# Dealing the steps of an expert lookup over the units of a decoder block's last part

## The reference

```python
q = jnp.einsum('bnd,de->bne', x, w_q)
mean = jnp.mean(q, axis=(0, 1)); var = jnp.var(q, axis=(0, 1))
q = (q - mean) * jax.lax.rsqrt(var + BN_EPS) * bn_gamma + bn_beta
q = q.reshape(b, n, 2, H, KD).transpose(2, 0, 1, 3, 4)
sim = jnp.einsum('pbnhd,hkpd->pbnhk', q, keys)
sx, ix = jax.lax.top_k(sim[0], TOPK)
sy, iy = jax.lax.top_k(sim[1], TOPK)
all_scores = (sx[..., :, None] + sy[..., None, :]).reshape(b, n, H, TOPK * TOPK)
all_indices = (ix[..., :, None] * NUM_KEYS + iy[..., None, :]).reshape(b, n, H, TOPK * TOPK)
scores, pk = jax.lax.top_k(all_scores, TOPK)
indices = jnp.take_along_axis(all_indices, pk, axis=-1)
wd = down_embed[indices]
wu = up_embed[indices]
h = gelu_new(jnp.einsum('bnd,bnhkd->bnhk', x, wd))
h = jax.nn.softmax(scores, axis=-1) * h
out = jnp.einsum('bnhk,bnhkd->bnd', h, wu)
```

## Time and profile before

| | us |
|---|---|
| median of 3 runs | 2746.43 (2737.4 to 2747.01) |
| profiled execution | 2732.75, span 2730.9 |
| first gather issued | 1358.2 |
| gathers of head 7 begin | 2555.1 |
| last gather issued | 2714.4 |
| TensorE busy | 2356.3 (86%) |
| VectorE busy | 1869.2 (68%) |
| ScalarE busy | 1176.5 (43%) |
| GpSimd busy | 1144.1 (42%) |

### The profile page before, as it was taken

How to read it: one execution, slowest core, us unless ns; L and a number is a source line. 1 busy time by engine, 2 the same in 40 slices (tenths; PEclk the granted TensorE clock), 3 DMA queues, 4 the chain that set the end, 5 groups by cost and what they waited for, 6 DMA issues and landing times.

```text
span 2730.9 us, 37792 instructions
## 1 busy us (share of the span) xinstructions
PE 2356.3 (86%) x12444; PEld 1259.1 (46%) x12444; DVE 1869.2 (68%) x5474; ACT 1176.5 (43%) x3224; POOL 1144.1 (42%) x1082
## 2 busy tenths in 40 slices
PE   8999999999999999998868888778878788876767
PEld 4565555656555565655534433333333343332323
DVE  4676777777687777768467767677775766766554
ACT  3365574736557473657223423323333332332222
POOL 3111212111121211120166576676667666577665
PEclk9999999999999999999989999989899998898889
DMA  4001001010100101011189899999999999899998
GB/s 175 30 1 37 8 8 37 1 44 1 41 4 10 36 1 43 1 60 58 58 320 364 299 369 357 349 354 345 358 352 363 351 362 358 309 359 356 355 375 330
DMA packets 161954, 521.78 MB, mean 191 GB/s; under 512 B 17248, under 2 KB 27488, under 8 KB 161760
## 3 DMA queue, kind: packets, MB, share of 16 engines
q0 software_dynamic: 129024, 469.82, 45.8%
q1 hardware_dynamic: 31152, 48.03, 5.3%
q10 hardware_dynamic: 1584, 1.52, 0.2%
HBM read 508.30 MB, written 11.01 MB: 190 GB/s over the span
## 4 chain that ended last, share of the span: by engine, by line
PE 20%; issue 10%; DVE 10%; another core or an unknown queue 3%; POOL 3%; DMA 3%; ACT 1%; DVEq 1%; POOLq 0%; ACTq 0%
PE ps_y L1819 7%; PE ps_o L1819 7%; DVE e_rows L1965 5%; PE ps_s L1789 3%; POOL e_rows L1769 3%; DMA e_rows<-in_experts,e_idx 3%; PE ps_t L1802 1%; ACT e_diag L2047 1%; DVE acc L1955 1%; DVE e_at L1899 1%; DVE e_best_at L1879 1%; DVEq L1903 0%; DVE q_stats L1847 0%; ACT e_q_t L2022 0%
## 5 line engine op out<-in xcount | busy, mean ns | idle before, releaser
L1769 POOL DMA_INDIRECT e_rows<-in_experts,e_idx x896 | 908.6, 1014 | 473.0 <-issue 284.6
L1965 DVE CUSTOM_DVE_ANT_0 e_rows<-e_rows,xn_all 128x512 f32<-128x512 f32 x896 | 568.6, 688 | 148.4 <-DMA e_rows<-in_experts,e_idx 112.5
L1819 PE MATMUL ps_o<-e_rows,e_diag 128*128 128x512 f32 x896 | 443.1, 642 | 149.2 <-issue 131.3
L1819 PE MATMUL ps_y<-e_rows,e_diag 128*128 128x512 f32 x896 | 434.5, 632 | 121.6 <-ACT e_diag L2047 60.4
L2047 ACT ACTIVATE e_diag<-ident_f,e_weight 128x128 f32<-128x128 f32 x896 | 286.3, 390 | 560.5 <-DVE e_weight L1976 197.1
L1819 PEld LDWEIGHTS ps_o<-e_rows,e_diag 128*128 128x128 f32 x896 | 179.8, 206 | 384.7 <-issue 362.5
L1819 PEld LDWEIGHTS ps_y<-e_rows,e_diag 128*128 128x128 f32 x896 | 178.1, 203 | 355.1 <-issue 316.1
L1133 DVE SCALAR_TENSOR_TENSOR ring<-ps_s,mask 112x750 f32<-112x750 f32 x248 | 225.0, 936 | 129.2 <-PE ps_s L624 110.1
L1359 ACT ACTIVATE ring<-ring,neg_max 112x750 f32<-112x750 f32 x248 | 226.8, 916 | 157.6 <-DVE neg_max L1143 157.2
L1143 DVE CUSTOM_DVE_ANT_0 ring<-ring,mask_bias 112x750 f32<-112x750 f32 x248 | 233.5, 989 | 0.0
L2042 ACT ACTIVATE e_active<-e_hidden 128x4 f32<-128x4 f32 x224 | 45.6, 204 | 359.5 <-DVE e_hidden L1965 143.3
(11 more groups left out here) (226 smaller groups left out, 3189.8 us busy)
## 6 DMA issues: line engine op xcount, KB each, us to landing
e_rows<-in_experts,e_idx POOLq DMA_INDIRECT x896
xn_t<-in_ctx_t SPq DMA_DIRECT2D x8, 1500.0 KB, 6.7
w_in<-in_ffn_wq SPq DMA_DIRECT2D x16, 256.0 KB, 7.6
acc<-in_x SPq DMA_DIRECT2D x8, 448.0 KB, 4.9
acc<-x_dram SPq DMA_DIRECT2D x7, 512.0 KB, 6.5
xn_all<-x2n_dram SPq DMA_DIRECT2D x7, 512.0 KB, 7.1
out<-acc SPq DMA_DIRECT2D x14, 256.0 KB
x_dram<-x SPq DMA_DIRECT2D x7, 448.0 KB, 3.1
```

The lines of the kernel that those rows point to most:

```text
L1769: pool.indirect_dma_start(rows[:, v % RING, k, :], None, table[:, :], bass.IndirectOffsetOnAxis(ap=idx[:, e:e + 1], axis=0))\
L1819: mm = nc.tensor.matmul(ps_out[t % 2][:], diag[:, HU * (v % ND) + k, :], rows[:, v % RING, k, D:], start=(s == 0 and k == 0), stop=(s == S ...
L1965: last = nc.vector.tensor_tensor_reduce(down, down, xn_all[:, t, :], 1.0, 0.0, ALU.mult, ALU.add, hidden[:, b, k:k + 1])
```

## The change

`steps_in` is looked up in a table, DEAL, that is built once. Head 1's steps stand as before. From head 2 on the 40 steps of a head are dealt evenly over 28 units, 1 or 2 a unit: step k of head j stands in unit 21 + k * 28 // 40, counted from the start of head j - 2. So they begin in unit 21 of head j - 2 and end in unit 20 of head j - 1, and the next head's begin right behind them. No unit carries steps of two heads. Where a unit has two steps, they are done in order. Nothing else is changed, and each engine does the same instructions in the same order of steps within one head.

In a head h of 1 to 5 the units then carry, of head h + 1: unit 0 steps 10 and 11, 1: 12, 2: 13 and 14, 3: 15, 4: 16 and 17, 5: 18, 6: 19, 7: 20 and 21, 8: 22, 9: 23 and 24, 10: 25, 11: 26 and 27, 12: 28, 13: 29, 14: 30 and 31, 15: 32, 16: 33 and 34, 17: 35, 18: 36 and 37, 19: 38, 20: 39; and of head h + 2: unit 21 steps 0 and 1, 22: 2, 23: 3 and 4, 24: 5, 25: 6 and 7, 26: 8, 27: 9.

```diff
--- before.py
+++ after.py
@@ -1672,25 +1672,24 @@
         ACT_STEPS = {9: [("root", 0, 0)], 10: [("affine", 0, 0)], 21: [("root", 1, 0)], 22: [("affine", 1, 0)],
                      35: [("soften", 0, 0)]}
         N_STEPS = 40
-        LEAD = 20
+        LAST_AT = 20
         AHEAD = 2 * QC
         FIRST_TURNS = [0, *(min(N_STEPS, AHEAD + 2 + 3 * v // 2) for v in range(NV))]
-        SECOND_TURNS = [0, 1, 2, 3, 4, 5, 6, 7, 8, 10, 12, 13, 14, 15, 16, 17, 18, 20]
-        SECOND_AT = NV - len(SECOND_TURNS) + 1
+
+        def unit_of(head, k):
+
+            if head == 1:
+                return max(v for v in range(NV) if FIRST_TURNS[v] <= k)
+            return NV * (head - 1) - (NV - LAST_AT) + 1 + k * NV // N_STEPS
+
+        DEAL = {}
+        for head in range(1, HF):
+            for k in range(N_STEPS):
+                DEAL.setdefault(unit_of(head, k), []).append((head, k))
 
         def steps_in(h, v):
 
-            if h == 0:
-                found = [(1, k) for k in range(FIRST_TURNS[v], FIRST_TURNS[v + 1])]
-                if v >= SECOND_AT:
-                    found += [(2, k) for k in range(SECOND_TURNS[v - SECOND_AT], SECOND_TURNS[v - SECOND_AT + 1])]
-                return found
-            found = []
-            if h + 1 < HF and v + LEAD < N_STEPS:
-                found.append((h + 1, v + LEAD))
-            if h + 2 < HF and v >= NV - LEAD:
-                found.append((h + 2, v - NV + LEAD))
-            return found
+            return DEAL.get(NV * h + v, ())
 
         def two_before(h, t):
```

## The result

| | old order | new order |
|---|---|---|
| median, range, runs | 2743.36 us (2737.4 to 2747.01), 4 | 2781.30 us (2772.85 to 2797.52), 4 |
| profiled execution, span | 2732.75, 2730.9 | 2778.78, 2777.0 |

The ratio is 1.0147, 95% interval 1.0096 to 1.0199: the new order is 38 us slower, 46 us in the profiled executions. The forecast was +11 (2757), the range 2715 to 2795.

A forecast was written before the change was run, and what follows sets the result against it. Gathers at 409 GB/s bound it, standing still at head ends where the 6-slot ring is four deep. Terms 10.5 + 2.5 - 1.7 gave +11 us, put on the runs' median 2746.43: 2757, range 2715 to 2795.

The forecast's parts named there:

- rival (a): Units 18 to 20: TensorE drops to its low clock after idling, 4 us a head, +31, 2777 us; chance 0.20.
- with holes moved by one a head: Allowance in the range for unexplained engine standstills of 8 to 17 us falling elsewhere, one a head.
- Units 14 to 24: VectorE's start of 14 to TensorE's end of 24: 2.1 us later a head, five times, 10.5 in all.
- Unit 25: Two projecting steps on TensorE delay the gathers into unit 1's slot: 0.5 us a head, 2.5 in all.
- Heads 1 to 5: The two terms of these heads, 10.5 and 2.5 us, together 13.0 us slower.
- head 0: First head: counts and an affine leave VectorE's units 14 to 20, so 1.7 us faster.
- head 6: No projecting after unit 20 in either order, so VectorE's later finish is recovered before unit 24: nothing.
- four-deep boundary: Units 0 to 3 reuse slots four units back; half a microsecond of slack, so TensorE's lag at unit 24 idles transfers.
- Units 1 to 6: TensorE carries 35.7 us against 30.8 of transfers; the 4.9 lag is hidden by the six-deep ring: nothing.
- Rival (b): Lighter units 7 to 13 let TensorE win back lag from holes: -18 us, 2728; chance 0.22.
- Rival (c): Holes swallow the shift and the gathers' time stays hidden as before: no change, 2746 us; chance 0.12.
- GpSimd's wait ahead of unit 0: Sign at each head's start: GpSimd waits 6 us or more before issuing unit 0's gathers.

The follow-up runs named there:

- quiet runs: Both orders unchanged, in later jobs whose traces have hardly any holes (engines standing together): new order 2598.25 us, 14.6 more than the old, ratio 1.0051.
- experiment 5: New order with a 7.6 us VectorE stall in unit 10 alone: 2605.24 us; in units 2 and 10, second half's projecting cut to 64 columns: 2602.66.
- two other dealings: Against the old order: the new order itself, ratio 1.0051 without holes, and the even dealing with its last step in unit 14, 2589.05 us, ratio 1.0018.

## Why the prediction was right in the small and short in the size

- **The range.** 2781 lies in 2715 to 2795, 24 us above the forecast. The range reached so far because it took in rival (a) at 2777, "with holes moved by one a head". (a) is not what happened. Holes in another place are a part of it, but the sum has no term for them. That the first comparison's time lies inside is luck for the most part; what the forecast's own sum describes is the quiet runs, +11 against 14.6 (9 to 18).
- **Units 14 to 24, +2.1 a head.** Right in kind and somewhat small. From VectorE's start of unit 14 to TensorE's end of unit 24 it was +3.2 in the quiet traces (67.5 and 64.2 us) and +1.1 in the first; unit 14 starting 0.4 earlier, unit 24 ended 2.8 later, which is all that a head got longer. The term that was off is VectorE's units 14 to 20 in the new order, 40.1 us instead of 38.0 (14 to 19 in the old one: 32.4 instead of 31.7).
- **Unit 25, +0.5.** Its step is there, 3.9 - 2.8 = 1.1 more at TensorE and 0.9 more ahead of unit 1's gathers, but 0.3 are left at unit 3's and nothing at VectorE's unit 14. So the 2.6 came near 2.9 partly because one term was small and the other cost nothing.
- **Heads 1 to 5, 13.0 us in all; the whole, +11.** In quiet runs 14.3 and +14.6. The other parts there, from the spans: head 0 -3.5 (forecast -1.7), head 6 -1.0 (0), from head 7's first gather on +0.6 (0), and 4.1 ahead of the first gather (1359.6 instead of 1355.5), where both orders do the same. Over all fourteen traces the first gather goes out between 1355.5 and 1361.1 us in either order, and head 0 takes most of this up: head 1's gathers begin at 1518.7 and 1519.3. So head 0's -3.5 can't be put down to the change, and all that these parts add is 0.2.
- **The mechanism of the four-deep boundary.** Shown: with the ring carried through, 14.6 becomes 2.9, and each order gains what GpSimd had waited there.
- **Units 1 to 6: "nothing".** This is the step that was mis-sized. Its numbers were right (35.7 us against 30.8; units 3 to 6 took 23.0), and so was its condition, "with the cover gone, as after a stall of more than 6 us, what is over costs one for one". The mistake was to price it as if the cover were free, when the same trace showed an engine standing some 8 to 17 us in every head. With two stalls of 7.6 us a head its value is not 0 but 4.9 ((44.6 - 10.1) / 7, experiment 5). In the first comparison the new order lost 5.8 a head ahead of unit 14; with the 1.1 of the stretch behind it that is 6.9, and 6.8 were measured. How much of the 5.8 is this step is not shown: what stands at unit 10, 2.8, may be it; the rest came with a hole in unit 10 that the old order's trace doesn't have. Why the holes fell there, and whether they would again, stays open. The made stalls also stop only VectorE.
- **Rival (a), the clock.** Its sign was there and its price was not: unit 18's products took a mean of 6.0 us instead of 4.6 in the quiet traces (over 5 us in five of five heads, before in three), but units 19 and 20 gave it back, and TensorE's end of unit 20 is 9.1 us after VectorE's start in the new order, 10.3 in the old. In the first comparison the whole stretch from unit 14 to 24 was only 1.1 longer.
- **Rival (b), TensorE catches up.** It does: in the first comparison TensorE's lag behind the old order falls from 7.0 us at the end of unit 6 to 0.2 at the end of unit 9. What (b) left out is the hole in unit 10, and that units 1 to 6 are heavier. Its -18 didn't come.
- **Rival (c), nothing:** false, at 1.0147 and at 1.0051.
- GpSimd's wait ahead of unit 0, forecast at 6 or more, was 9.7, 6.2, 2.1, 7.5 and 6.9 us in the first trace; heads 1 to 5 took 169 to 179 us, not 171 to 172, and head 0 189.5, not 182 or 183.

## What to carry to other kernels

A buffer's depth is a cover with two customers, the load that you put under it and the stalls that the trace already has. Take both off before you call a load hidden. And look at what an order does right behind a stall: units lighter than the transfers' pace win time back, heavier ones keep the lag alive until the next stall comes on top. Where a ring's length doesn't divide the loop, count the slots through the loops; that gained 9 us here, and neither of the two other dealings gained anything by itself.

## What was not expected of the hardware

The same old order took 2743 us in the first comparison and 2584 in four later jobs on three chips. In the view of waits the new order's first trace has rows of this kind for VectorE:

```profile
DVE e_best L1875 <- remote: 99.0, 25, 10.0
DVE e_best L1875 <- issue: 40.1, 9, 9.3
DVE e_weight L1975 <- issue: 34.1, 43, 5.3
```

and the quiet trace of the very same kernel has none of them; what is left for nothing shown in the lookup steps is 2.0 us:

```profile
DVE e_best_at L1878 <- issue: 1.6, 5, 0.4
DVE e_top L1892 <- issue: 0.4, 1, 0.4
```

So the holes belong to the circumstances of the run, not to the program alone. The amount of code that is streamed doesn't explain them: both pages of the profile show the same transfers for it,

```profile
q8 instruction: 100, 1.64, 0.3%
...
q14 instruction: 94, 0.77, 0.1%
```

(the quiet one's). Nor did these transfers take longer: behind the first gather those of q8 took a mean of 1.08 us and those of q14 0.33 in the first trace, 1.06 and 0.33 in the quiet one. How long an engine waits ahead of such a transfer isn't shown, so streaming is unlikely as the cause and not ruled out. By the Trainium skill, Runtime: NRT & Kernel Launch, section Instruction fetch mechanics, crossing into the next block is mostly hidden; the quiet trace agrees, with 2.0 us of unexplained waiting on VectorE's lookup steps. What makes the holes is open; nothing that I ran brought them back, and whether the first comparison's chip or its surroundings did it can't be told from these runs.
